# Second layer's gated convolution: the difference and the gate product move from GpSimd to VectorE, the first tap from VectorE to ScalarE, and two tiles stand ahead of the softmax

## The chip, the cores and the metric

One core of a Trainium2 chip runs the whole program. The metric is the time of one execution on the device in microseconds (us). Below, PE is TensorE, DVE is VectorE, ACT is ScalarE, POOL is GpSimd and SP is SyncE; all numbers are float32.

## What is computed

Two layers, one after the other, work on 4 x 512 tokens of width 128. The change lies in the second layer's mixer, which works on 256 hidden channels:

```python
    u = jnp.einsum('bld,hd->blh', x, W_x) + b_x
    g = jax.nn.sigmoid(jnp.einsum('bld,hd->blh', x, W_g) + b_g)
    h = conv(u, conv_w) + conv_b            # per channel, 3 taps along the tokens
    u = u * g + h * (1.0 - g)
    dt = softplus(einsum('bld,hd->blh', x, W_dt) + b_dt).mean(axis=(0, 1)); dt = clip(dt, 0.001, 2.0)
    A = -softplus(A_raw)
    A_d = exp(A * dt[:, None]); B_d = (A_d - 1.0) / (A + 1e-06) * B_ssm
    # state = A_d * state + B_d * u_t ; y_t = sum(state * C_ssm)
    y = scan(u); return layernorm(x + y @ W_out.T + b_out)
```

Beside the mixer, the second layer has a mixture of 8 experts (softmax gate, best two of eight), and the result is the sum of both and of the input.

## The kernel before

The second layer is one block of the program (`layer1`), in which each engine has its own list of instructions written out by hand; counters (semaphores) hold an engine until another has come far enough. Nothing is reordered: what stands first on an engine runs first.

The tokens are worked on in `NU` = 8 tiles, n = 0 to 7: batch row n // 2 (512 tokens, along the free dimension) and half n % 2 of the 256 channels (on 128 partitions). For one tile:

- PE makes u, the gate and dt products (`u_product`, `gate_product`, `dt_product`).
- ACT copies u from PSUM into `ub` with its bias (`u_tile`, L1564), makes the gate by a sigmoid (L1589), and for dt an absolute value and a relu (L1599, L1602; a softplus in two parts).
- DVE makes the convolution in `cv`, one instruction for each tap (`conv`: L1716, L1718, L1721), and, later in its list, the sum `uT = cv + df` (`blend`, L1728).
- POOL stands between the two: `df = ub - cv` (L1867) and `df = df * gate` (L1870).

`ub`, `cv` and `df` have two places each, used in turn. The profile shows them all as "region", since they are parts of one tensor.

Around the tiles, DVE's list holds the gates of the experts (`gates`: softmax, best two; L1672 to L1691), four copies (`gate_rows`, L1696) and products with the gates of the experts (`apply_gate`, L1701). The order before is: conv(0), conv(1), gates, blend(0), then for n = 2 to 7 conv(n) and blend(n - 1) with the smaller pieces between, and blend(7) last. Then come two transposes of all of `uT` (L1755), and a chain of short instructions that makes dt (L1758 to L1765) and `lna` (L1766), the logarithm of the state's decay. It needs the end of the softplus from ACT (`ln_done`, raised at L1618). For `lna` the rest waits: on ACT, exponentials (L1620, L1622) and then the activations of the next experts (`hidden`, L1557), on PE the products of these experts (`up`, L1396, `picks`, `down`), and after them the matrices of the scan (L1631 to L1646).

POOL's list in this block is: clear `gt` (L1858), add a bias to `xt` (L1861), the eight pairs L1867 and L1870, add `out_b` to `xn1` (L1871), clear region2 once `ln_done` is 2 (L1873), and at the very end parts of the last sums.

Of the kernel before, what the change touches and what calls it, by code (L numbers as in the profile page):

```python
# [11 lines left out]
ACT = mybir.ActivationFunctionType  # L12
ALU = mybir.AluOpType
# [3 lines left out]
B, L, D = 4, 512, 128  # L17
# [80 lines left out]
def build(nc, a, const, out):  # L98
    ctx = ExitStack()
    with ctx, nc.allow_non_contiguous_dma(reason="bias columns and token regrouping"):  # L100
# [39 lines left out]
        with ExitStack() as until_layer1:  # L140
# [1144 lines left out]
def layer1(nc, a, out, g):  # L1285
# [13 lines left out]
    a_raw, b_ssm, c_ssm, cw, cb = m1.a_raw, m1.b_ssm, m1.c_ssm, m1.cw, m1.cb  # L1299
    NBC = B * NCH  # L1300
    NU = 2 * B
    with ExitStack() as c:
        uT = sb("uT", [P, 2, TOK], c=c)
# [5 lines left out]
        gate = region1[:, :].rearrange("p (n l) -> p n l", n=NU)  # L1309
# [9 lines left out]
        ub = region3[:, 0:W].rearrange("p (n l) -> p n l", n=2)  # L1319
        cv, df = (region3[:, W + 2 * L * i:W + 2 * L * (i + 1)].rearrange("p (n l) -> p n l", n=2) for i in range(2))  # L1320
# [23 lines left out]
        S = lambda *names: tuple(sem(n, c) for n in names)  # L1344
# [1 line left out]
            "gate_mm", "mx_done", "ex_done", "gates_done", "gt_mm", "gT_done", "moe_order")  # L1346
        up_mm, pick_mm, he_done, gated, down_mm, y_done = S("e_up", "e_pick", "he_done", "gated", "e_down", "y_done")
        w_mm, w_done, pads, u_mm, g_mm, dt_mm = S("mix_tr", "mix_cp", "pads", "u_mm", "g_mm", "dt_mm")
        u_done, gate_done, conv_done, diff_done, blend_in, uT_done = S(
            "u_done", "gate_done", "conv_done", "diff_done", "blend_in", "uT_done")  # L1350
        abs_done, relu_done, exp_done, ln_done = S("abs_done", "relu_done", "exp_done", "ln_done")

        a_stage, lna_done, t1_done, kex_stage = S("a_stage", "lna_done", "t1_done", "kex_stage")
# [11 lines left out]
        row = lambda b: slice(b * L, (b + 1) * L)  # L1365
# [19 lines left out]
        with nc.Block() as block:  # L1385
# [165 lines left out]
            def _(act):  # L1551
# [7 lines left out]
                def u_tile(n):  # L1559
                    act.wait_ge(u_mm, n + 1)  # L1560
                    if n >= 2:
                        act.wait_ge(conv_done, 3 * (n - 1))
                        act.wait_ge(diff_done, n - 1)
                    nc.scalar.activation(ub[:, n % 2, 1:L + 1], bank[n % 2][:, :], ACT.Identity, bias=m1.bx[:, n % 2:n % 2 + 1]).then_inc(u_done, 1)  # L1564

                def tap_blocks(q):

                    nc.scalar.activation(wtap[quad(q), :, quad(q)], x2[quad(q), :, :].rearrange("p c j -> p j c"),  # L1568
                                         ACT.Copy).then_inc(taps, 1)
# [26 lines left out]
                for n in range(NU):  # L1596
                    b, k = divmod(n, 2)
# [66 lines left out]
            def _(dve):  # L1664
# [29 lines left out]
                def gate_rows(k):  # L1694
                    dve.wait_ge(gt_mm, k + 1)
                    nc.vector.tensor_copy(gT[:, k * 512:(k + 1) * 512], bank[6 + k % 2][:, :]).then_inc(gT_done, 1)  # L1696

                def apply_gate(n):
                    dve.wait_ge(he_done, n + 1)
                    dve.wait_ge(pick_mm, n + 1)  # L1700
                    nc.vector.tensor_tensor(he[:, n % 8, :], he[:, n % 8, :], pick_bank(n // 4, n % 4)[:, :], ALU.mult).then_inc(gated, 1)  # L1701
# [6 lines left out]

                def conv(n):

                    b, k = divmod(n, 2)
                    p = n % 2
                    dve.wait_ge(u_done, n + 1)
                    if n >= 2:
                        dve.wait_ge(uT_done, n - 1)
                    nc.vector.tensor_scalar(cv[:, p, :], ub[:, p, 0:L], cw[:, k, 0:1], cb[:, k:k + 1], ALU.mult, ALU.add).then_inc(conv_done, 1)  # L1716
                    dve.wait_ge(conv_done, 3 * n + 1)
                    nc.vector.scalar_tensor_tensor(out=cv[:, p, :], in0=ub[:, p, 1:L + 1], scalar=cw[:, k, 1:2], in1=cv[:, p, :],  # L1718
                                                   op0=ALU.mult, op1=ALU.add).then_inc(conv_done, 1)
                    dve.wait_ge(conv_done, 3 * n + 2)  # L1720
                    nc.vector.scalar_tensor_tensor(out=cv[:, p, :], in0=ub[:, p, 2:L + 2], scalar=cw[:, k, 2:3], in1=cv[:, p, :],  # L1721
                                                   op0=ALU.mult, op1=ALU.add).then_inc(conv_done, 1)

                def blend(n):

                    b, k = divmod(n, 2)
                    dve.wait_ge(blend_in, n + 1)
                    nc.vector.tensor_tensor(uT[:, k, row(b)], cv[:, n % 2, :], df[:, n % 2, :], ALU.add).then_inc(uT_done, 1)  # L1728


                sc = Chain(dve, v_order)
# [4 lines left out]
                nc.vector.tensor_tensor(asp[:], asp[:], a_raw[:], ALU.max).then_inc(a_stage, 1)  # L1736
                w(nc.vector.tensor_scalar(bsp[:], a_raw[:], 0.0, None, ALU.max))
                conv(0)
                conv(1)
                gates()  # L1740
                blend(0)
                for n in range(2, NU):
                    conv(n)
                    blend(n - 1)
                    if n in (2, 3):
                        gate_rows(2 * n - 4)
                        gate_rows(2 * n - 3)
                    if n >= 6:
                        apply_gate(2 * n - 12)
                        apply_gate(2 * n - 11)  # L1750
                blend(NU - 1)
                dve.wait_ge(uT_done, NU)
                for i in range(2):
                    half_n = slice(i * NBC // 2, (i + 1) * NBC // 2)
# [55 lines left out]
                for m in range(8):  # L1810
# [3 lines left out]
                    n = 512 - (m == 7)  # L1814
# [41 lines left out]
            @block.gpsimd  # L1856
            def _(pool):
                nc.gpsimd.memset(gt, 0.0).then_inc(pool_stage, 1)  # L1858
                pool.wait_ge(m1.w_in, 16 * m1.loads)

                nc.gpsimd.tensor_tensor(xt[:], xt[:], m1.lnb[:, None, :].broadcast_to([P, NT, D]), ALU.add).then_inc(pool_stage, 1)  # L1861
                for n in range(NU):
                    p = n % 2
                    pool.wait_ge(conv_done, 3 * n + 3)
                    if n >= 2:
                        pool.wait_ge(uT_done, n - 1)
                    nc.gpsimd.tensor_tensor(df[:, p, :], ub[:, p, 1:L + 1], cv[:, p, :], ALU.subtract).then_inc(diff_done, 1)  # L1867
                    pool.wait_ge(diff_done, n + 1)
                    pool.wait_ge(gate_done, n + 1)
                    nc.gpsimd.tensor_tensor(df[:, p, :], df[:, p, :], gate[:, n, :], ALU.mult).then_inc(blend_in, 1)  # L1870
                nc.gpsimd.tensor_tensor(xn1[:], xn1[:], m1.out_b[:, None, :].broadcast_to([P, NT, D]), ALU.add).then_inc(pool_stage, 1)  # L1871
                pool.wait_ge(ln_done, 2)
                nc.gpsimd.memset(region2[:], 0.0).then_inc(pool_stage, 1)  # L1873
                for m in range(2):
                    scale_add(nc, pool, m)
# [35 lines left out]
```

## Time and profile before

| | |
|---|---|
| median of 3 runs | 486.31 us (486.05 to 487.7) |
| the profiled execution's own time | 487.49 us |
| its span, from first to last instruction | 485.7 us, so 1.79 us lie around it |
| second layer's block | about 332 us to 485.7 us of the span |
| busy in the span: PE, DVE, ACT, POOL | 390.9, 307.6, 291.9, 196.3 us |
| mean granted clock of PE | 0.911 of full speed |

The profile lists for every instruction when it ran, how long, and what its engine had waited for. A duration includes time in which an instruction had begun and could not proceed. Two instructions on one engine overlap by some 0.1 us when the second does not need the first's result, so the distance between two starts is often a little less than the duration.

### The profile page before, as it was taken

The page shows a single profiled execution, that of the slowest core. Times are in us where ns is not written, and L with a number is a line of the kernel's source. Part 1 is how long each engine was busy: PE and PEld are TensorE (multiplying, and loading weights), DVE is VectorE, ACT ScalarE, POOL GpSimd, SP SyncE. Part 2 cuts the span into 40 slices and gives each one's busy share as a digit, 9 for nine tenths or more (in the row PEclk, how much of TensorE's full clock was granted, in tenths as well). Part 3 has the DMA queues.
Part 4 walks back from the last instruction along what each step waited for, and adds up shares of the span by engine and source line. Part 5 has one row for each costly group of instructions (what it writes and reads, how often), then busy time and mean ns, then how long its engine had stood idle before and what let it go on. Part 6 is the DMA issues. An engine that isn't in the chain of part 4 may idle for free. (4 is left out here: it accounts for less than half of the span.)

```text
span 485.7 us, 10292 instructions
## 1 busy us (share of the span) xinstructions
PE 390.9 (80%) x3168; PEld 266.0 (55%) x3168; DVE 307.6 (63%) x1066; ACT 291.9 (60%) x707; POOL 196.3 (40%) x279
## 2 busy tenths in 40 slices
PE   0799999986999999999970999973898456785990
PEld 0443444335777777777750577762543142665890
DVE  4664726333777777777761357777489896365096
ACT  1266858583666677666651446663578925696634
POOL 1001736403588888888863600005415760000003
PEclk9999999998899999999995579995899876997996
DMA  8120223243122222222123510000000001000003
GB/s 232 22 49 28 67 68 98 69 120 119 42 57 62 65 60 64 65 65 65 49 84 90 118 21 1 2 0 1 0 1 1 1 0 23 1 1 1 0 1 86
DMA packets 35355, 23.06 MB, mean 47 GB/s; under 512 B 10478, under 2 KB 35068, under 8 KB 35324
## 3 DMA queue, kind: packets, MB, share of 16 engines
q1 hardware_dynamic: 34908, 22.55, 17.3%
q8 instruction: 15, 0.25, 0.2%
q10 hardware_dynamic: 416, 0.13, 0.1%
q14 instruction: 16, 0.13, 0.1%
HBM read 13.20 MB, written 9.47 MB: 47 GB/s over the span
## 5 line engine op out<-in xcount | busy, mean ns | idle before, releaser
L449 PE MATMUL bank<-w,hT 128*128 128x385 f32 x128 | 45.6, 496 | 0.6 <-ACT stage L577 0.6
L906 ACT ACTIVATE win<-bank 128x384 f32<-128x384 f32 (+1 forms) x124 | 43.1, 399 | 0.0
L835 PE MATMUL bank<-win,wst 128*32 128x128 f32 x1024 | 42.7, 282 | 0.0
L449 PEld LDWEIGHTS bank<-w,hT 128*128 128x128 f32 x128 | 23.2, 189 | 25.0 <-issue 12.7
L1167 ACT ACTIVATE std_<-mv_,cst 128x2 f32<-128x2 f32 (+1 forms) x46 | 13.5, 296 | 37.2 <-DVE mv_ L1147 20.3
L1380 POOL TENSOR_TENSOR win<-win,lng 128x512 f32<-128x512 f32 x2 | 2.5, 1265 | 77.1 <-ACT win L1661 77.1
L835 PEld LDWEIGHTS bank<-win,wst 128*32 128x32 f32 x1024 | 25.3, 110 | 8.0 <-issue 0.6
L1396 PE MATMUL bank<-xn1T,w1e 128*128 128x512 f32 x32 | 17.7, 676 | 12.4 <-ACT he L1557 12.1
L973 POOL TENSOR_SCALAR xh<-raw,bmv,brs 128x128 f32<-128x128 f32 x32 | 25.4, 793 | 3.0 <-DVE brs L1025 2.9
L830 PE MATMUL bank<-win,cst 128*128 128x128 f32 x128 | 25.6, 283 | 0.7 <-DVE grad L1072 0.7
L966 POOL TENSOR_TENSOR xkm<-win,wst 128x256 f32<-128x256 f32 x32 | 19.6, 613 | 15.0 <-PE bank L852 12.7
L911 ACT ACTIVATE zstd<-zmv,cst 128x1 f32<-128x1 f32 x32 | 9.4, 294 | 26.5 <-DVE zmv L1049 26.5
L1858 POOL MEMSET region<- 128x2048 f32 x1 | 1.8, 1806 | 58.2 <-POOLq L1110 58.2
L576 ACT ACTIVATE stage<-bank 128x384 f32<-128x384 f32 x32 | 15.5, 485 | 11.7 <-PE bank L449 11.2
L852 PE MATMUL bank<-grad,xkm 32*128 32x128 f32 x496 | 22.5, 296 | 0.0
L958 POOL TENSOR_TENSOR gd<-wst,win 128x128 f32<-128x128 f32 x32 | 13.8, 432 | 21.4 <-POOLq L295 21.4
L1867 POOL TENSOR_TENSOR region<-region 128x512 f32<-128x512 f32 x8 | 11.9, 1492 | 25.4 <-DVE region L1721 25.4
L1217 PE MATMUL bank<-region,tT 128*128 128x256 f32 x64 | 21.9, 472 | 0.0
L422 DVE TENSOR_TENSOR move<-tw,coup 128x512 f32<-128x512 f32 x8 | 8.7, 1090 | 20.2 <-ACT coup L609 20.2
L1203 PE MATMUL bank<-cst,yn 128*128 128x128 f32 x32 | 8.0, 340 | 16.2 <-ACT yn L1184 14.2
L830 PEld LDWEIGHTS bank<-win,cst 128*128 128x128 f32 x128 | 20.1, 198 | 1.0 <-DVE grad L1072 0.9
L852 PEld LDWEIGHTS bank<-grad,xkm 32*128 32x128 f32 x496 | 16.6, 185 | 3.7
(300 smaller groups left out, 1193.6 us busy)
## 6 DMA issues: line engine op xcount, KB each, us to landing
rows_scratch<-stage SPq DMA_DIRECT2D x32, 192.5 KB
win<-rows_scratch SPq DMA_DIRECT2D x32, 192.5 KB, 2.4
attn_scratch<-ob SPq DMA_DIRECT2D x32, 64.0 KB, 1.6
att<-attn_scratch SPq DMA_DIRECT2D x32, 64.0 KB
xt<-in_L_attn_x SPq DMA_DIRECT2D x4, 256.0 KB, 5.9
out<-win SPq DMA_DIRECT2D x4, 256.0 KB, 2.4
cst<-in_constants SPq DMA_DIRECT2D x1, 535.5 KB, 4.3
w<-in_L_attn_wk SPq DMA_DIRECT2D x2, 128.0 KB, 4.9
```

What stands on the lines that cost most here:

```text
L449: mm = nc.tensor.matmul(rows_bank(i, h)[:, 0:RC], hT[:, k, i * P:(i + 1) * P], w4[:, k, h, :], start=(k == 0), stop=(k == 1))
L576: act.activation(stage[:, i % 2, h, 0:3 * F], src[:, 0:3 * F], ACT.Copy).then_inc(stage_done[h], 1)
L830: nc.tensor.matmul(dst[:, 0:F], con("ident"), w_sb[:, state, 2, :], start=True, stop=False, skip_group_check=True)
L835: mm = nc.tensor.matmul(dst[32 * b:32 * b + 32, 0:F], v[:, at:at + 2 * K], w_sb[:, state, first_slot(b) + h, :], start=False, stop=(h == 1 ...
L852: mm = nc.tensor.matmul(bank[b][:, h * F:(h + 1) * F], xkm[own, p % 2, h, :], grad[own, p % 2, :], start=False, stop=False, skip_group_che ...
L906: nc.scalar.activation(w_sb[:, state, at:at + n, :], bank[b][:, 0:n * F].rearrange("f (h g) -> f h g", h=n), ACT.Copy).then_inc(w_done, 1)
L958: nc.gpsimd.tensor_tensor(gd[:], grf[:], rows[:, p, F:2 * F], ALU.mult).then_inc(gd_done, 1)
L966: nc.gpsimd.tensor_tensor(xkm[:, p % 2, :, :], rows[:, p, 0:F][:, None, :].broadcast_to([P, H, F]), headt[:, :, None].broadcast_to([P, H, ...
L973: nc.gpsimd.tensor_scalar(xh[:], raw[:, p % 2, :], bmv[:, 0:1], brs[:, 0:1], ALU.subtract, ALU.mult).then_inc(xg_done, 1)
L1167: nc.scalar.activation(std[:, p, ks], mv[:, p, ks, 1], ACT.Sqrt, bias=con("eps5")).then_inc(std_done, 1)
L1217: ins = nc.tensor.matmul(dst, tT[:, 1 - p, 0, k * P:(k + 1) * P], wo[:, k, :], start=False, stop=(k == 1))
L1396: nc.tensor.matmul(bank[4 + n % 2][:, :], m1.w1[:, q, :], xn1T[:, tok], start=True, stop=True).then_inc(up_mm, 1)
```

## The change

The first tap is now an activation on ACT, right behind the copy of u, in `u_tile`. DVE makes taps two and three, and then, in the new `blend`, the difference, the product with the gate and the sum, all for the same tile. POOL does nothing for the tiles. Tiles 0 and 1 are finished ahead of `gates`. The counters are renumbered for this.

```diff
@@ ScalarE, u_tile(n)
                     if n >= 2:
-                        act.wait_ge(conv_done, 3 * (n - 1))
-                        act.wait_ge(diff_done, n - 1)
+                        act.wait_ge(conv_done, 2 * (n - 1))
+                        act.wait_ge(diff_done, 2 * n - 3)
                     nc.scalar.activation(ub[:, n % 2, 1:L + 1], bank[n % 2][:, :], ACT.Identity, bias=m1.bx[:, n % 2:n % 2 + 1]).then_inc(u_done, 1)
+                    act.wait_ge(u_done, n + 1)
+                    if n >= 2:
+                        act.wait_ge(uT_done, n - 1)
+                    nc.scalar.activation(cv[:, n % 2, :], ub[:, n % 2, 0:L], ACT.Identity, bias=cb[:, n % 2:n % 2 + 1],
+                                         scale=cw[:, n % 2, 0:1]).then_inc(tap_done, 1)
@@ VectorE, conv(n): the first tap goes, the other two stay
-                    dve.wait_ge(u_done, n + 1)
-                    if n >= 2:
-                        dve.wait_ge(uT_done, n - 1)
-                    nc.vector.tensor_scalar(cv[:, p, :], ub[:, p, 0:L], cw[:, k, 0:1], cb[:, k:k + 1], ALU.mult, ALU.add).then_inc(conv_done, 1)
+                    dve.wait_ge(tap_done, n + 1)
...
@@ VectorE, blend(n)
-                    dve.wait_ge(blend_in, n + 1)
-                    nc.vector.tensor_tensor(uT[:, k, row(b)], cv[:, n % 2, :], df[:, n % 2, :], ALU.add).then_inc(uT_done, 1)
+                    dve.wait_ge(conv_done, 2 * n + 2)
+                    nc.vector.tensor_tensor(df[:, p, :], ub[:, p, 1:L + 1], cv[:, p, :], ALU.subtract).then_inc(diff_done, 1)
+                    dve.wait_ge(diff_done, 2 * n + 1)
+                    dve.wait_ge(gate_done, n + 1)
+                    nc.vector.tensor_tensor(df[:, p, :], df[:, p, :], gate[:, n, :], ALU.mult).then_inc(diff_done, 1)
+                    dve.wait_ge(diff_done, 2 * n + 2)
+                    nc.vector.tensor_tensor(uT[:, k, row(b)], cv[:, p, :], df[:, p, :], ALU.add).then_inc(uT_done, 1)
@@ VectorE, the order
                 conv(0)
+                blend(0)
                 conv(1)
+                blend(1)
                 gates()
-                blend(0)
                 for n in range(2, NU):
                     conv(n)
-                    blend(n - 1)
+                    blend(n)
...
-                blend(NU - 1)
@@ GpSimd
-                for n in range(NU):
-                    p = n % 2
-                    pool.wait_ge(conv_done, 3 * n + 3)
-                    if n >= 2:
-                        pool.wait_ge(uT_done, n - 1)
-                    nc.gpsimd.tensor_tensor(df[:, p, :], ub[:, p, 1:L + 1], cv[:, p, :], ALU.subtract).then_inc(diff_done, 1)
-                    pool.wait_ge(diff_done, n + 1)
-                    pool.wait_ge(gate_done, n + 1)
-                    nc.gpsimd.tensor_tensor(df[:, p, :], df[:, p, :], gate[:, n, :], ALU.mult).then_inc(blend_in, 1)
```

The lists of the engines show it as follows (the changed kernel has its own line numbers). First GpSimd's list, before, with the last of the eight pairs (the other seven stand ahead of it, and the clearing L1858 and the addition L1861 ahead of them):

```order
L1867 TENSOR_TENSOR region<-region 128x512 [waits uT_done,conv_done]
L1870 TENSOR_TENSOR region<-region 128x512 [waits gate_done,diff_done]
L1871 TENSOR_TENSOR xn<-xn,out_b 128x2048
L1873 MEMSET region 128x4096 [waits ln_done]
L1380 TENSOR_TENSOR win<-win,lng 128x512 [waits zn_done]
```

And GpSimd's list in the changed kernel, from the block's first clearing on:

```order
L1864 MEMSET region 128x2048
L1867 TENSOR_TENSOR xt<-xt,lnb 128x2048 [waits l1_weights]
L1868 TENSOR_TENSOR xn<-xn,out_b 128x2048
L1870 MEMSET region 128x4096 [waits ln_done]
L1380 TENSOR_TENSOR win<-win,lng 128x512 [waits zn_done]
```

The addition of `out_b` has moved up to right behind the addition to `xt`, with no wait between them, and the clearing of region2 now waits for `ln_done` alone.

Next ScalarE's list from tile 6's copy of u to the first exponential of the softplus, before:

```order
L1564 ACTIVATE region<-bank,bx 128x512 [waits diff_done,conv_done,u_mm]
L1557 ACT_TABLE_LOAD
L1557 ACTIVATE he<-bank,b1e 128x512 [waits e_up] x2
L1564 ACTIVATE region<-bank,bx 128x512 [waits diff_done,conv_done,u_mm]
L1557 ACTIVATE he<-bank,b1e 128x512 [waits e_up] x2
L1613 ACT_TABLE_LOAD
L1613 ACTIVATE region<-region 128x4096 [waits abs_done]
```

And the same place in the changed kernel:

```order
L1564 ACTIVATE region<-bank,bx 128x512 [waits diff_done,conv_done,u_mm]
L1568 ACTIVATE region<-region,cb,cw 128x512 [waits uT_done,u_done]
L1557 ACT_TABLE_LOAD
L1557 ACTIVATE he<-bank,b1e 128x512 [waits e_up] x2
L1564 ACTIVATE region<-bank,bx 128x512 [waits diff_done,conv_done,u_mm]
L1568 ACTIVATE region<-region,cb,cw 128x512 [waits uT_done,u_done]
L1557 ACTIVATE he<-bank,b1e 128x512 [waits e_up] x2
L1618 ACT_TABLE_LOAD
L1618 ACTIVATE region<-region 128x4096 [waits abs_done]
```

Each copy of u is followed by a tap (L1568), with no table load between; everything behind, the softplus included, stands one instruction further back per tile.

Last VectorE's list at the end of the tiles, from conv(7) to the sum in which `ln_done` is waited for, before:

```order
L1716 TENSOR_SCALAR region<-region,cw,cb 128x512 [waits uT_done,u_done]
L1718 SCALAR_TENSOR_TENSOR region<-region,cw 128x512 [waits conv_done]
L1721 SCALAR_TENSOR_TENSOR region<-region,cw 128x512 [waits conv_done]
L1728 TENSOR_TENSOR uT<-region 128x512 [waits blend_in]
L1701 TENSOR_TENSOR he<-he,bank 128x512 [waits e_pick,he_done] x2
L1728 TENSOR_TENSOR uT<-region 128x512 [waits blend_in]
L1755 STREAM_TRANSPOSE region<-uT 128x64x32 [waits uT_done]
L1755 STREAM_TRANSPOSE region<-uT 128x64x32
L1758 TENSOR_REDUCE dt<-dtr 128x2
L1761 TENSOR_TENSOR asp<-bsp,asp 128x32 [waits a_stage,ln_done,ssm_v]
```

And the same place in the changed kernel:

```order
L1718 SCALAR_TENSOR_TENSOR region<-region,cw 128x512 [waits tap_done]
L1721 SCALAR_TENSOR_TENSOR region<-region,cw 128x512 [waits conv_done]
L1729 TENSOR_TENSOR region<-region 128x512 [waits conv_done]
L1732 TENSOR_TENSOR region<-region 128x512 [waits gate_done,diff_done]
L1734 TENSOR_TENSOR uT<-region 128x512 [waits diff_done]
L1706 TENSOR_TENSOR he<-he,bank 128x512 [waits e_pick,he_done] x2
L1761 STREAM_TRANSPOSE region<-uT 128x64x32 [waits uT_done]
L1761 STREAM_TRANSPOSE region<-uT 128x64x32
L1764 TENSOR_REDUCE dt<-dtr 128x2
L1767 TENSOR_TENSOR asp<-bsp,asp 128x32 [waits a_stage,ln_done,ssm_v]
L1768 TENSOR_TENSOR dt<-dt,dtl 128x2
L1769 TENSOR_SCALAR asp<-asp 128x32 [waits ssm_v]
```

A tile is now five instructions of which each needs the one before it, and the last sum no longer stands alone ahead of the transposes.

## Rows read from the trace of the kernel before

**Rows 1.** Chain of work that ended last: start us, us, what.

```profile
388.18 5.02 DVE uT L1728
...
405.06 5.68 PE bank L1396 x8
```

**Rows 2.** Timeline of GpSimd in the second layer: start us, us, instruction.

```profile
332.75 1.81 POOL L1858 MEMSET region<- 128x2048 f32 x1 [58.18 <-POOLq L1110]
334.52 4.49 POOL L1861 TENSOR_TENSOR xt<-xt,lnb 128x2048 f32<-128x2048 f32 x1
...
373.59 1.33 POOL L1870 TENSOR_TENSOR region<-region 128x512 f32<-128x512 f32 x1
...
388.12 4.52 POOL L1871 TENSOR_TENSOR xn<-xn,out_b 128x2048 f32<-128x2048 f32 x1
392.58 3.50 POOL L1873 MEMSET region<- 128x4096 f32 x1
```

**Rows 3.** Timeline of VectorE, 333 to 402 us.

```profile
333.86 0.72 DVE L1735 TENSOR_SCALAR asp<-a_raw 128x32 f32<-128x32 f32 x1
334.62 4.43 DVE L1736 TENSOR_TENSOR asp<-asp,a_raw 128x32 f32<-128x32 f32 x1
...
344.01 0.75 DVE L1718 SCALAR_TENSOR_TENSOR region<-region,cw 128x512 f32<-128x512 f32 x1
344.80 0.75 DVE L1721 SCALAR_TENSOR_TENSOR region<-region,cw 128x512 f32<-128x512 f32 x1
...
352.52 0.29 DVE L1672 TENSOR_REDUCE mx<-bank 128x16 f32<-128x128 f32 x1 [3.17 <-PE bank L1483]
...
359.39 0.69 DVE L1728 TENSOR_TENSOR uT<-region 128x512 f32<-128x512 f32 x1
...
366.95 0.68 DVE L1728 TENSOR_TENSOR uT<-region 128x512 f32<-128x512 f32 x1
367.55 1.28 DVE L1696 COPY ffnT<-bank 128x512 f32<-128x512 f32 x2
...
373.83 1.64 DVE L1718 SCALAR_TENSOR_TENSOR region<-region,cw 128x512 f32<-128x512 f32 x1
...
400.27 0.14 DVE L1758 TENSOR_REDUCE dt<-dtr 128x2 f32<-128x8 f32 x1
...
400.77 0.18 DVE L1763 TENSOR_SCALAR asp<-asp 128x32 f32<-128x32 f32 x1
...
401.26 0.19 DVE L1766 TENSOR_TENSOR lna<-asp,dt 128x32 f32<-128x32 f32 x1
```

**Rows 4.** Waits of the second layer: who waited for whom, total us, times, longest.

```profile
ACT t L1620 <- DVE lna L1766: 10.2, 1, 10.2
...
ACT region L1564 <- POOL region L1867: 2.4, 2, 1.4
```

**Rows 5.** Timeline of ScalarE: first layer (53 to 56 us), then the second.

```profile
53.87 0.69 ACT L603 ACTIVATE tanh<-bank,half_b 128x512 f32<-128x512 f32 x1
54.59 0.81 ACT L609 ACTIVATE coup<-tanh,alpha,beta 128x512 f32<-128x512 f32 x1
55.31 0.47 ACT L576 ACTIVATE stage<-bank 128x384 f32<-128x384 f32 x1
...
369.05 0.69 ACT L1564 ACTIVATE region<-bank,bx 128x512 f32<-128x512 f32 x1
369.62 0.69 ACT L1599 ACTIVATE region<-bank,bd 128x512 f32<-128x512 f32 x1
...
389.83 0.19 ACT L1618 ACTIVATION_READ_ACCUMULATOR region<-region 128x1 f32 x1
...
430.58 1.98 ACT L1568 ACTIVATE region<-region 32x1024 f32<-32x1024 f32 x1
```

**Rows 6.** Windows: length, busy us of PE, PEld, DVE, ACT, POOL (instructions), granted PE clock, DMA.

```profile
396.00:399.00 3.00, 0.00 (x0) 0.00 (x0) 3.00 (x2) 0.00 (x0) 0.09 (x1) 0.97 0.00 0
...
405.00:409.00 4.00, 3.94 (x5) 1.80 (x6) 3.77 (x10) 1.39 (x4) 0.00 (x0) 0.50 0.13 45
```

More of the change, by code:

```diff
@@ L1348, in layer1 @@
         w_mm, w_done, pads, u_mm, g_mm, dt_mm = S("mix_tr", "mix_cp", "pads", "u_mm", "g_mm", "dt_mm")
-        u_done, gate_done, conv_done, diff_done, blend_in, uT_done = S(
-            "u_done", "gate_done", "conv_done", "diff_done", "blend_in", "uT_done")
+        u_done, gate_done, conv_done, diff_done, tap_done, uT_done = S(
+            "u_done", "gate_done", "conv_done", "diff_done", "tap_done", "uT_done")
         abs_done, relu_done, exp_done, ln_done = S("abs_done", "relu_done", "exp_done", "ln_done")
@@ L1709, in conv @@
                 def conv(n):
-                    b, k = divmod(n, 2)
-                    p = n % 2
-                    dve.wait_ge(u_done, n + 1)
-                    if n >= 2:
-                        dve.wait_ge(uT_done, n - 1)
-                    nc.vector.tensor_scalar(cv[:, p, :], ub[:, p, 0:L], cw[:, k, 0:1], cb[:, k:k + 1], ALU.mult, ALU.add).then_inc(conv_done, 1)
-                    dve.wait_ge(conv_done, 3 * n + 1)
+                    k, p = n % 2, n % 2
+                    dve.wait_ge(tap_done, n + 1)
                     nc.vector.scalar_tensor_tensor(out=cv[:, p, :], in0=ub[:, p, 1:L + 1], scalar=cw[:, k, 1:2], in1=cv[:, p, :],
                                                    op0=ALU.mult, op1=ALU.add).then_inc(conv_done, 1)
-                    dve.wait_ge(conv_done, 3 * n + 2)
+                    dve.wait_ge(conv_done, 2 * n + 1)
                     nc.vector.scalar_tensor_tensor(out=cv[:, p, :], in0=ub[:, p, 2:L + 2], scalar=cw[:, k, 2:3], in1=cv[:, p, :],
@@ L1726, in blend @@
                     b, k = divmod(n, 2)
-                    dve.wait_ge(blend_in, n + 1)
-                    nc.vector.tensor_tensor(uT[:, k, row(b)], cv[:, n % 2, :], df[:, n % 2, :], ALU.add).then_inc(uT_done, 1)
+                    p = n % 2
+                    dve.wait_ge(conv_done, 2 * n + 2)
[5 more added lines that the diff above has]
+                    nc.vector.tensor_tensor(uT[:, k, row(b)], cv[:, p, :], df[:, p, :], ALU.add).then_inc(uT_done, 1)
                 sc = Chain(dve, v_order)
@@ L1861, in _ @@
                 nc.gpsimd.tensor_tensor(xt[:], xt[:], m1.lnb[:, None, :].broadcast_to([P, NT, D]), ALU.add).then_inc(pool_stage, 1)
-                for n in range(NU):
-                    p = n % 2
-                    pool.wait_ge(conv_done, 3 * n + 3)
-                    if n >= 2:
-                        pool.wait_ge(uT_done, n - 1)
-                    nc.gpsimd.tensor_tensor(df[:, p, :], ub[:, p, 1:L + 1], cv[:, p, :], ALU.subtract).then_inc(diff_done, 1)
-                    pool.wait_ge(diff_done, n + 1)
-                    pool.wait_ge(gate_done, n + 1)
-                    nc.gpsimd.tensor_tensor(df[:, p, :], df[:, p, :], gate[:, n, :], ALU.mult).then_inc(blend_in, 1)
                 nc.gpsimd.tensor_tensor(xn1[:], xn1[:], m1.out_b[:, None, :].broadcast_to([P, NT, D]), ALU.add).then_inc(pool_stage, 1)
```

## The prediction

> **What bounds the kernel now.** I read the chain of work that ended last first. Through the tiles it is GpSimd's two instructions of each tile and the DVE work between them; then one DVE sum, 0.68 us long elsewhere [rows 3], stands for 5.02 us [rows 1]. The timeline of GpSimd says why: the addition of out_b began at 388.12 and ran 4.52 us [rows 2], just ahead of that sum at 388.18. The same shows in the small: a tap that takes 0.75 us alone took 1.64 us from 373.83, while GpSimd's product ran from 373.59 for 1.33 us [rows 2, 3]. So DVE instructions that read two tensors stand still while a GpSimd tensor_tensor runs. The table of waits says what hangs on the tiles: ACT had been idle for 10.2 us when lna came [rows 4], written from 401.26 [rows 3]. From there the chain goes to PE at 405.06 [rows 1] and on, through PE, ACT and DVE in turn, to the end, each step released by the one before. Lna's time is thus the time of all that follows, and I ask when lna is written in the changed kernel.
>
> **The change, on DVE.** A tile is five dependent instructions. Tap to its dependent is 344.80 - 344.01 = 0.79 us; a tensor_tensor to its dependent is 0.68 + 0.04 (the gap between these taps) = 0.72; to an independent one 367.55 - 366.95 = 0.60 [rows 3]. So tap, tap, difference, product, sum: 0.79 + 0.79 + 0.72 + 0.72 + 0.60 = 3.62 us, now that no GpSimd work lies beside it. The softmax starts at 352.52, after 3.17 us of waiting for PE's router products [rows 3], which in PE's order follow sigmoids of ACT, and a tap now stands ahead of these: +0.83 us (next paragraph), 353.35. Tiles 0 and 1 lie ahead of it: from about 344.1 (where tap two of tile 0 stood, 344.01 [rows 3], and it waits for ACT's tap) two tiles, 7.24 us, and some 1.3 us of waiting for the first sigmoid, to 352.7. That wait of DVE is what hides them, with 0.6 us to spare; beyond that each us is added in full. Conv(2) thus starts where blend(0) stood, 359.39 [rows 3], plus 0.83 = 360.22. Then six tiles, 21.72 us, and eight small instructions (four copies, four products) of 0.60, 4.80 us: the transposes start at 386.74. From the blend's end to the reduction was 400.27 - (388.18 + 5.02) = 7.07 us [rows 1, 3], so the reduction is at 393.8 instead of 400.27: **6.5 us earlier**.
>
> **The change, on ACT.** The tap has a near twin in the first layer, an activation with scale and bias columns from SBUF, 128x512: 0.81 us, 0.72 after the instruction whose result it needs, and 0.72 ahead of the next [rows 5]. A copy of u alone holds the queue for 369.62 - 369.05 = 0.57 [rows 5]; with its tap 1.44, so +0.87 a tile, or +0.83 where a table load, which does not overlap, follows (1.53 for 0.70). Along ACT's list to the softplus: tap 1 +0.83 and tap 2 +0.83, ahead of the sigmoids; tap 3 hidden in a wait for PE's dt product; tap 4 +0.87; tap 5 +0.75 (0.12 in another wait for PE); taps 6 and 7 +0.83 and +0.86; tap 0 hidden in a wait for PE. That is 4.97. Against it, ACT's two waits for GpSimd go, 2.4 us [rows 4] and twice the 0.12 us of overlap that they broke. So the last accumulator read of the softplus, 389.83 + 0.19 [rows 5], moves to about 390.0 + 2.3 = 392.3 us. That is still ahead of DVE's 393.8, and no tap holds DVE up (tap 6 is the nearest, done at 376.9 for a tile that starts at 377.1).
>
> **The change, on GpSimd.** The addition of out_b moves to about 339.0, behind that to xt [rows 2], and beside it DVE has only one short instruction, not needed until the first tile at 344. The clearing of region2 used to run from 392.58 for 3.50 us [rows 2], beside transposes. Now it starts with ln_done, at 392.4, and ends at 395.9, so it lies on the chain that makes dt and lna. Does a clearing hold DVE up? One row bears on it: the 128x32 tensor_scalar at 333.86 took 0.72 us, and 0.18 elsewhere [rows 3], and it ended (334.58) just as GpSimd's clearing ended (332.75 + 1.81 = 334.56) [rows 2]. I take that: the tensor_scalar L1763, ready 0.50 us after the reduction, at 394.3, stands until about 395.75, a new wait of **1.45 us**. Lna follows 0.49 later, at 396.25, instead of 401.26.
>
> The Trainium skill's page SBUF — State Buffer, section "Who interferes with whom", says that VectorE and GpSimd share a pair of ports under an exclusive lock. A tensor_scalar in a two-port mode meets any GpSimd instruction there, and one with two SBUF inputs only those that read SBUF. By that rule the clearing blocks L1763 but not L1761 and L1762 ahead of it, and lna comes at 396.25; the short tensor_scalar at 333.86 agrees, and nothing here shows the second half. The page ScalarE: Activation LUTs, section "Rules for kernel authors", budgets some 0.3 us and 0.83 ns an element for an activation, an estimate of 0.72 us for a tap; the rows say 0.81, and with 0.72 the sum would be some 0.6 us lower.
>
> **The sum.** -6.5 on DVE, +1.45 behind the clearing: -5.0 us. After lna nothing changes but, it may be, PE's clock. Before, PE had nothing to do after 396, its clock was at 0.97 of 2.4 GHz up to 399, and from 405 to 409 it worked 3.94 us at 1.2 GHz [rows 6]. It now restarts at about 400. I take it to be at 1.2 GHz then too, and nothing gained; at the full clock those 3.94 us would be half as long, -2.0 us at most. The profiled execution would go from 487.49 to 482.5; it stood 1.2 us above the median, and from the median of 486.31 I come to **481.3 us**.
>
> Bounds of the unknown prices. The clearing: 0 (it ran beside transposes with no loss) to 1.45. The tap: 0.69, as the copy of u, to 0.81; below, ln_done comes some 0.8 us earlier, and so the end of the clearing (-0.8). Tiles 0 and 1 ahead of the softmax: 0 to +1. A tap on ACT at 1.98, the longest such row [rows 5], is a rival below. With PE's clock these give 479.3 to 482.5.
>
> **Rivals.**
> 1. *The clearing does not block.* For it: transposes ran beside it. Against it: the tensor_scalar at 333.86. Then DVE decides, -6.5: 479.8 us. Chance 0.12.
> 2. *The early addition starves asp.* DVE's L1736 stood 4.43 us behind the addition to xt [rows 3], and ACT's list begins with its result. If GpSimd's next addition, now right behind, is served first, L1736 waits a further 4.5 us and all of the layer moves: 481.3 + 4.5 = 485.8 us. Against it: the tensor_scalar at 333.86 got in between GpSimd's clearing and the addition behind it. Chance 0.06.
> 3. *ACT becomes the bound: slower.* If a tap cost 1.98 us, as the strided copy at 430.58 [rows 5], 1.17 more each, the six or seven taps that count would put ln_done, and the clearing behind it, 7 to 8 us later: 489 us. It decides from a tap of about 1.6 us on. The twin at 0.81 speaks against it. Chance 0.02.
> 4. *The gain does not carry.* Something behind lna (the round trip of lna through DRAM, a product) was due then anyway: 486.3 us. Against it: ACT's idle 10.2 us ahead of lna, and a chain in which each step starts as the last ends. Chance 0.05.
>
> **How the numbers follow.** Forecast 0.75, rivals 0.12, 0.06, 0.02, 0.05. A difference of 0.3%, 1.46 us, is about what this measurement tells from none. Faster: forecast and rival 1, 0.87. Within: rivals 2 and 4, 0.11. Slower: rival 3, 0.02. The range holds the bounds and rival 1 and, above, 1 us more for tiles 0 and 1 or losses that no row shows: 479.3 to 483.5.
>
> **What would show it.** On DVE, eight tiles of 3.6 us with no tap above 0.8, the transposes at about 386.7, and the tensor_scalar behind them at 1.5 us, ending with the clearing. On ACT, taps of 0.81 us, no wait for GpSimd or VectorE in the tiles, the last accumulator read at 392.3, and the wait for lna about 2.5 us instead of 10.2. On GpSimd, the addition of out_b at 339. Wrong would be: asp written at 343.5 (rival 2); a softmax that starts later than 353.4 (tiles 0 and 1 not covered); a clearing that ends with no DVE instruction behind it (rival 1); or an lna at 396 with a span that is not 5 us shorter (rival 4).

## The result, and the profile after the change

Five runs each (the kernel before has two more than above, and the same median): 482.47 us (481.17 to 483.01) against 486.31 us before (486.05 to 487.7), a ratio of 0.991 with a 95% interval of 0.9889 to 0.9931. The change makes the kernel 3.8 us faster; the forecast was 481.3 us, with a range of 479.3 to 483.5. The profiled execution took 482.47 us too.

The top of the page after the change:

```profile
span 480.7 us, 10286 instructions
...
PE 390.9 (81%) x3168; PEld 265.9 (55%) x3168; DVE 308.6 (64%) x1074; ACT 298.3 (62%) x715; POOL 173.1 (36%) x263
```

GpSimd has 23 us less to do and ACT 6 us more. The chain of work that ended last, from the softplus on (start us, us, what), answers to [rows 1]:

```profile
387.43 3.80 ACT region L1623 x4
...
391.26 1.66 DVE region L1761
...
393.27 1.55 DVE asp L1769
...
395.08 0.20 DVE lna L1772
...
398.14 0.70 ACT he L1557
...
398.88 6.46 PE bank L1396 x8
```

The sum that stood 5.02 us behind GpSimd is gone from it. A clearing's wait (L1769, 1.55 us) is in it now, and the next products of experts on PE, behind lna, take 6.46 us (x8: four products, each with two records). The timeline of GpSimd, as [rows 2]:

```profile
333.28 4.49 POOL L1867 TENSOR_TENSOR xt<-xt,lnb 128x2048 f32<-128x2048 f32 x1
337.73 4.51 POOL L1868 TENSOR_TENSOR xn<-xn,out_b 128x2048 f32<-128x2048 f32 x1
391.27 3.51 POOL L1870 MEMSET region<- 128x4096 f32 x1 [49.03 <-ACT region L1623]
```

And that of VectorE, as [rows 3]: behind the early addition, at the softmax, in a tile, and at the end of the tiles:

```profile
333.38 4.44 DVE L1742 TENSOR_TENSOR asp<-asp,a_raw 128x32 f32<-128x32 f32 x1
337.74 4.53 DVE L1743 TENSOR_SCALAR bsp<-a_raw 128x32 f32<-128x32 f32 x1
...
352.13 0.29 DVE L1677 TENSOR_REDUCE mx<-bank 128x16 f32<-128x128 f32 x1 [0.39 <-PE bank L1483]
...
368.65 0.74 DVE L1718 SCALAR_TENSOR_TENSOR region<-region,cw 128x512 f32<-128x512 f32 x1
369.43 0.75 DVE L1721 SCALAR_TENSOR_TENSOR region<-region,cw 128x512 f32<-128x512 f32 x1
370.22 0.69 DVE L1729 TENSOR_TENSOR region<-region 128x512 f32<-128x512 f32 x1
370.94 0.69 DVE L1732 TENSOR_TENSOR region<-region 128x512 f32<-128x512 f32 x1
371.67 0.69 DVE L1734 TENSOR_TENSOR uT<-region 128x512 f32<-128x512 f32 x1
372.28 0.74 DVE L1718 SCALAR_TENSOR_TENSOR region<-region,cw 128x512 f32<-128x512 f32 x1
...
385.55 7.37 DVE L1761 STREAM_TRANSPOSE region<-uT 128x2048 f32<-128x2048 f32 x2
392.77 0.15 DVE L1764 TENSOR_REDUCE dt<-dtr 128x2 f32<-128x8 f32 x1
392.98 0.19 DVE L1767 TENSOR_TENSOR asp<-bsp,asp 128x32 f32<-128x32 f32 x1
393.09 0.15 DVE L1768 TENSOR_TENSOR dt<-dt,dtl 128x2 f32<-128x2 f32 x1
393.27 1.55 DVE L1769 TENSOR_SCALAR asp<-asp 128x32 f32<-128x32 f32 x1
...
395.08 0.19 DVE L1772 TENSOR_TENSOR lna<-asp,dt 128x32 f32<-128x32 f32 x1
```

A tile takes 372.28 - 368.65 = 3.63 us. L1769 is held until the clearing ends (391.27 + 3.51 = 394.78), while the two-input L1767 and L1768 just ahead of it ran through it unhindered. ScalarE, as [rows 5], and its wait for lna, as [rows 4] (who waited for whom: total us, times, longest):

```profile
370.36 0.69 ACT L1564 ACTIVATE region<-bank,bx 128x512 f32<-128x512 f32 x1
371.08 0.81 ACT L1568 ACTIVATE region<-region,cb,cw 128x512 f32<-128x512 f32 x1
371.80 0.67 ACT L1604 ACTIVATE region<-bank,bd 128x512 f32<-128x512 f32 x1
...
391.03 0.18 ACT L1623 ACTIVATION_READ_ACCUMULATOR region<-region 128x1 f32 x1
```

```profile
ACT t L1625 <- DVE lna L1772: 2.8, 1, 2.8
```

Windows behind lna (columns as in [rows 6]):

```profile
396.00:399.00 3.00, 0.12 (x1) 0.12 (x1) 0.69 (x4) 2.77 (x4) 0.00 (x0) 0.77 0.25 38
399.00:405.00 6.00, 6.00 (x8) 2.30 (x8) 5.21 (x13) 2.37 (x4) 0.00 (x0) 0.54 0.12 27
405.00:409.00 4.00, 4.00 (x32) 2.97 (x32) 0.69 (x1) 0.78 (x2) 0.00 (x0) 1.00 0.00 0
```

And the stretch in which PE's clock fell, ahead of these products:

```profile
397.00:398.00 1.00, 0.00 (x0) 0.00 (x0) 0.00 (x0) 1.00 (x1) 0.00 (x0) 0.82 0.09 33
398.00:399.00 1.00, 0.12 (x1) 0.12 (x1) 0.09 (x1) 0.99 (x3) 0.00 (x0) 0.50 0.49 66
```

The clock is down when PE's work behind lna begins at 398.88, and back within 404 to 405. That is some 5.6 us of work at 1.2 GHz; before it was four [rows 6].

**Where the time went.** The first layer is unchanged, yet its length differs between executions: the second layer's first instruction on VectorE (a memset) stands at 333.03 us before and 331.80 after, and at 330.4 to 333.2 in the profiles below. I therefore count from it. *Lna*: 401.26 - 333.03 = 68.23 us into the layer before, 395.08 - 331.80 = 63.28 after, **-4.95 us**. *Behind lna*, to the end of the span: 485.7 - 401.26 = 84.44 before, 480.7 - 395.08 = 85.62 after, **+1.18 us**. Together -3.77 us, and the medians differ by 3.84. That they agree so well is in part luck: a second measurement of both kernels ("changed, again" below) gave 482.19 against 487.25 us, 5.06 us less, while its profile has lna and the rest where the first had them. The medians alone put the gain between some 3 and 6 us; its terms are read from the profiles.

### The profile page after: what moved, and what is told of

The parts are those of the page before. It is cut to its first block and busy times, and to the rows that moved or that the text cites. A ratio compares the mean times of both kernels' runs of the same rounds, so it can differ in the third digit from the quotient of the medians.

```text
span 480.7 us, 10286 instructions
## 1 busy us (share of the span) xinstructions
PE 390.9 (81%) x3168; PEld 265.9 (55%) x3168; DVE 308.6 (64%) x1074; ACT 298.3 (62%) x715; POOL 173.1 (36%) x263
## 5 line engine op out<-in xcount | busy, mean ns | idle before, releaser
L966 POOL TENSOR_TENSOR xkm<-win,wst 128x256 f32<-128x256 f32 x32 | 19.6, 612 | 14.5 <-PE bank L852 12.4
L1870 POOL MEMSET region<- 128x4096 f32 x1 | 3.5, 3512 | 49.0 <-ACT region L1623 49.0
```

The source lines that it names most:

```text
L966: nc.gpsimd.tensor_tensor(xkm[:, p % 2, :, :], rows[:, p, 0:F][:, None, :].broadcast_to([P, H, F]), headt[:, :, None].broadcast_to([P, H, ...
```

## The experiments

In this table, "lna" is lna's start in us into the second layer, "behind" is from it to the span's end, "1.2 GHz" is PE's busy time behind lna at the lower clock (summed over windows of half a us, from busy time and granted clock; rough). "Lna" and "behind" come from one profile of each kernel. Each ratio is against the kernel before in the same set of runs.

| kernel | median us | ratio (95%) | lna | behind | 1.2 GHz |
|---|---|---|---|---|---|
| before | 486.31 | | 68.23 | 84.44 | 7.0 |
| changed | 482.47 | 0.991 (0.9889 to 0.9931) | 63.28 | 85.62 | 9.3 |
| changed, again | 482.19 | 0.9902 (0.987 to 0.9934) | 63.29 | 85.48 | 9.2 |
| e1: early addition alone | 481.08 | 0.9878 (0.9861 to 0.9896) | 63.73 | 84.45 | 7.1 |
| e2: clearing behind lna | 480.69 | 0.9866 (0.9849 to 0.9884) | 61.88 | 85.75 | 12.2 |
| e3: first tap on VectorE | 482.48 | 0.9915 (0.9891 to 0.9939) | 64.36 | 84.18 | 6.5 |
| e4: blends behind the softmax | 493.35 | 1.0115 (1.0097 to 1.0133) | 73.66 | 85.38 | 8.8 |
| e5: PE kept busy in one wait | 481.69 | 0.9903 (0.9866 to 0.994) | 63.09 | 84.86 | 7.6 |
| e6: late addition | 485.08 | 0.9958 (0.9932 to 0.9984) | 65.03 | 85.61 | 12.4 |
| e7: e1, a transpose behind lna | 480.08 | 0.9865 (0.9823 to 0.9907) | 60.64 | 86.9 | 13.2 |
| e8: changed, PE kept busy | 480.44 | 0.9868 (0.9835 to 0.99) | 63.10 | 83.01 | 0 |
| e9: e7, PE kept busy | 477.01 | 0.9788 (0.9757 to 0.9818) | 60.81 | 82.99 | 1.4 |
| e10: before, PE kept busy | 484.22 | 0.9932 (0.9906 to 0.9957) | 68.22 | 82.99 | 0 |
| e11b: both transposes behind lna | 476.6 | 0.9782 (0.9758 to 0.9807) | 57.62 | 84.34 | 4.2 |

My theory: lna's time sets the end, and it was late because of the addition; the rest of the change gives little more, since the clearing takes a part back. The rivals: the relief of GpSimd in the tiles, or the tap on ScalarE, is what gains. A second question came with the result: is the 1.18 us behind lna PE's clock?

### The addition of out_b alone (e1)

The kernel before, with GpSimd's addition moved ahead of its eight pairs:

```diff
                 nc.gpsimd.tensor_tensor(xt[:], xt[:], ...)
+                nc.gpsimd.tensor_tensor(xn1[:], xn1[:], m1.out_b...)
                 for n in range(NU):
...
-                nc.gpsimd.tensor_tensor(xn1[:], xn1[:], m1.out_b...)
```

> The kernel before, with one line moved: GpSimd adds out_b to xn1 ahead of the eight tiles instead of behind them; all else is as before. My theory (lna sets what follows, and the last sum of the tiles stood behind that addition): the sum needs 0.7 us instead of 5.0, the reduction starts about 4.3 us earlier in the second layer, the clearing now ends before it, lna is 4.3 us earlier, so about 482.0 us against 486.3; 1 us more or less with the time that PE spends at the lower clock after lna. Rival (the gain of the change comes from the 26 us of tiles in which GpSimd held up VectorE): little of it is here, 485 to 486 us.

Measured 481.08 us and lna at 63.73. One moved line brings lna forward by 4.5 us, and its median is no worse than that of the whole change. The clearing now runs under the transposes and ends 2.5 us before they do, so no instruction of the dt chain is held. In its timeline of VectorE:

```profile
386.40 7.30 DVE L1755 STREAM_TRANSPOSE region<-uT 128x2048 f32<-128x2048 f32 x2
393.55 0.15 DVE L1758 TENSOR_REDUCE dt<-dtr 128x2 f32<-128x8 f32 x1
...
394.06 0.18 DVE L1763 TENSOR_SCALAR asp<-asp 128x32 f32<-128x32 f32 x1
```

### The addition late again, in the changed kernel (e6)

```diff
+                pool.wait_ge(uT_done, 7)
                 nc.gpsimd.tensor_tensor(xn1[:], xn1[:], m1.out_b...)
```

> The changed kernel, but GpSimd's addition of out_b waits until tile 6 is blended, so it lies beside tile 7 as in the kernel before. Theory (such an addition stops every VectorE instruction that reads two tensors): the first tap of tile 7 on VectorE, due at 380.7, stands until the addition ends at about 384.1, so the transposes start 3.3 us later; the clearing is then over before the reduction and blocks nothing, which gives 1.4 us back: 2.0 us more than the changed kernel. Rival (the early place is worth nothing by itself): no difference.

It does what it did before the change, now to a tap. GpSimd, then VectorE:

```profile
378.37 4.52 POOL L1869 TENSOR_TENSOR xn<-xn,out_b 128x2048 f32<-128x2048 f32 x1 [41.73 <-DVE uT L1734]
```

```profile
379.40 4.04 DVE L1718 SCALAR_TENSOR_TENSOR region<-region,cw 128x512 f32<-128x512 f32 x1
```

A tap of 0.74 us stands 4.04. The transposes start 3.1 us later than in the changed kernel, lna comes 1.75 later (63.28 to 65.03; 2.0 were expected), since the clearing is then over before the tensor_scalar. The median is 2.9 us worse than the changed kernel's in the same set of runs (482.19 to 485.08). So the addition's place counts in both kernels. But it is not all of the gain: with the addition late, the rest of the change still has lna 3.2 us earlier than the kernel before (68.23 to 65.03). Only on top of an early addition does it give little (63.73 to 63.28).

### The clearing behind lna (e2)

```diff
-                pool.wait_ge(ln_done, 2)
+                pool.wait_ge(lna_done, 1)
                 nc.gpsimd.memset(region2[:], 0.0)
```

> The changed kernel, but GpSimd's clearing of region2 waits for lna instead of for the softplus. Theory (the clearing holds up VectorE's tensor_scalar ahead of lna): this tensor_scalar falls from 1.55 to 0.18 us, lna comes 1.4 us earlier, and the clearing now stands against instructions that have time, so 481.1 us where the changed kernel has 482.5. Rival (something else ended that wait, or the clearing now blocks the chain behind lna as long): 482.5 us or more.

VectorE, then GpSimd:

```profile
393.26 0.18 DVE L1769 TENSOR_SCALAR asp<-asp 128x32 f32<-128x32 f32 x1
...
393.75 0.19 DVE L1772 TENSOR_TENSOR lna<-asp,dt 128x32 f32<-128x32 f32 x1
...
394.75 2.80 DVE L1778 TENSOR_SCALAR asp<-asp 128x32 f32<-128x32 f32 x1
```

```profile
394.00 3.51 POOL L1870 MEMSET region<- 128x4096 f32 x1 [51.70 <-DVE lna L1772]
```

L1769 takes 0.18 us instead of 1.55 and lna comes 1.40 us earlier. The median of 480.69 (481.1 were expected) is 1.5 to 1.8 us below the two medians of the changed kernel; its interval lies clear of the first one's and overlaps with the second one's. The wait moved to the next tensor_scalar, 2.80 us, which is not due. Thus the new wait's price was 1.4 us, and the clearing blocks. The Trainium skill, page SBUF — State Buffer, section "Who interferes with whom", has both halves of this: a tensor_scalar in a two-port mode meets any GpSimd instruction, one with two SBUF inputs only those that read SBUF, and a clearing reads nothing. The changed kernel's trace agrees with the second half too: there L1767 and L1768 took 0.19 and 0.15 us in the clearing's midst.

### The first tap back on VectorE (e3)

```diff
@@ ScalarE, u_tile(n)
-                    nc.scalar.activation(cv[...], ub[...], ACT.Identity, bias=cb..., scale=cw...).then_inc(tap_done, 1)
@@ VectorE, conv(n)
+                    nc.vector.tensor_scalar(cv[...], ub[...], cw..., cb..., ALU.mult, ALU.add).then_inc(tap_done, 1)
```

> The changed kernel with the first tap back on VectorE; the difference and the product stay there, so a tile is six instructions on VectorE. Theory: a tile costs 4.20 instead of 3.62 us, 3.5 us more for the six tiles behind the softmax, which itself starts 0.8 us earlier as ScalarE has no tap ahead of the sigmoids; the softplus ends some 2 us earlier, so the clearing is over before the reduction and blocks nothing, 1.4 us less. Sum +1.3 us on the changed kernel: 483.8. Rival (ScalarE's longer list set the time of the changed kernel, through softplus and clearing): not slower than the changed kernel, 482.5 or less.

Lna is 1.08 us later (64.36), near what was expected, but the median is the same as the changed kernel's, not 1.3 us more, since less is lost behind lna (84.18 instead of 85.62). Without the tap ScalarE's softplus is done 3.1 us earlier and the clearing starts and ends under the transposes. So the tap on ScalarE is worth 64.36 - 61.88 = 2.5 us of lna where the clearing is out of the way, and 1.1 where it is not. And against e1, which has the first tap on VectorE too, the difference and the product on VectorE instead of GpSimd, with tiles 0 and 1 ahead of the softmax, bring lna no gain: 64.36 against 63.73. Both of the rivals fall as the one source of the gain: neither move gives the 4.95 us. As parts they stay, for without the early addition the two moves together are worth 3.2 us (e6).

### Blends of tiles 0 and 1 behind the softmax (e4)

```diff
                 conv(0)
-                blend(0)
                 conv(1)
-                blend(1)
                 gates()
+                blend(0)
+                blend(1)
```

> The changed kernel with the blends of tiles 0 and 1 behind the softmax, as tile 0's stood before. Theory (the order matters more than the placing, since ScalarE's next copy of u waits for the difference of tile 0 and stands ahead of four sigmoids and the whole of the softplus): ScalarE stands still for some 6 us, its whole list and the clearing move by as much, and lna comes about 6 us later: 488 us, slower than the kernel before. Rival (VectorE's own time is what counts, 2.1 us for each of two tiles): 486.7 us at most.

It was 493.35 us, where 488 were expected: the order does matter, and more than I had thought. Its timeline of ScalarE:

```profile
360.53 0.69 ACT L1564 ACTIVATE region<-bank,bx 128x512 f32<-128x512 f32 x1 [6.71 <-DVE region L1729]
361.96 0.81 ACT L1568 ACTIVATE region<-region,cb,cw 128x512 f32<-128x512 f32 x1 [0.74 <-DVE uT L1734]
...
366.94 0.69 ACT L1594 ACTIVATE region<-bank,bg 128x512 f32<-128x512 f32 x1 [1.59 <-PE bank L1455]
368.64 0.69 ACT L1594 ACTIVATE region<-bank,bg 128x512 f32<-128x512 f32 x1 [1.02 <-PE bank L1455]
370.35 0.69 ACT L1564 ACTIVATE region<-bank,bx 128x512 f32<-128x512 f32 x1 [1.02 <-PE bank L1449]
```

Tile 2's copy of u needs the difference of tile 0 (it overwrites `ub`), and stands 6.71 us for it, as the theory had it. Two things I had left out. Its tap waits another 0.74 us for tile 0's sum. And PE, whose products stand behind these sigmoids, had nothing to do for 7.79 us and came back at 1.2 GHz (its granted clock was 0.50 from 364 to 370 us), so that the next sigmoids and the next copy waited for PE. Counted from the layer's start, the tap is 7.4 us later than in the changed kernel, the next copy of u 10.0, and lna 10.4. The two tiles ahead of the softmax fill a wait of VectorE, and they also keep ScalarE and PE running.

### Is the loss behind lna PE's clock? (e5, e8, e10)

Products of which nothing is used (128x512, into a free bank) go into PE's waits. In e5 six of them stand behind `down(0)`, ahead of the products that wait for lna:

```diff
                     down(t - 1)
+                    if t == 1:
+                        for _ in range(6):
+                            nc.tensor.matmul(bank[1][:, :], con("ident"), xn1T[:, 0:512], start=True, stop=True)
```

> The changed kernel, with six products that nothing uses (128x512, into a free bank) on PE behind the first down product, in the 5.8 us in which PE waits for the experts' activation behind lna. Theory (PE worked 5.6 us at 1.2 GHz behind lna in the changed kernel, against 4.0 before, and that gave 0.8 us of the gain back): PE keeps 2.4 GHz through the wait, the expert products take 3.6 instead of 6.5 us, and VectorE's products with the gates set what follows, so the picks start 1.1 us earlier: 1.1 us less than the changed kernel. Rival (the clock there is off the path): no difference.

```profile
397.94 3.89 PE L1396 MATMUL bank<-xn1T,w1e 128*128 128x512 f32 x8 [0.54 <-ACT he L1560]
```

The four products behind lna took 3.89 us instead of 6.46, and the next step on PE (L1407, the picks) began 9.10 us behind lna instead of 10.19, as expected. But PE's clock fell again some 19.5 us behind lna (0.69 in 413 to 414 us, 0.50 in 414 to 416), and the median (481.69, interval 0.9866 to 0.994) can't be told from the changed kernel's: inconclusive by itself. So in e8 the changed kernel has such products in all four long waits behind lna (6, 1, 2 and 5 of them):

> The changed kernel with unused products on PE in four waits behind lna (6 behind the first down product, 1 ahead of the third picks, 2 ahead of the third down product, 5 ahead of the scan's output; each 128x512, 0.86 us at 2.4 GHz), all into banks that are free and each group shorter than its wait. Theory (the time from lna to the end, 85.6 us in the changed kernel against 84.4 before, is longer by PE's time at 1.2 GHz there, 9.3 us of busy time against 7.0): with 0 to 2 us at 1.2 GHz that time falls to 82.5 to 83.5 us and the kernel by 2 to 3 us. Rival (the clock's time is off the path or falls again elsewhere, as when only the first wait was filled): 85 us or more from lna to the end.

and in e10 the kernel before has them too (10, 1, 2 and 5):

> The kernel before, with the same unused products (10, 1, 2 and 5, as its first wait is 9.8 us). lna stays at 68.2 us into the layer. Theory (clock and lna are separate terms): from lna to the end falls from 84.4 to 82.5 to 83.5 us, so 1 to 2 us less than before. Rival (the clock costs only where lna is early): no difference.

Windows of e8:

```profile
396.00:399.00 3.00, 2.49 (x7) 0.94 (x6) 1.07 (x2) 2.40 (x3) 0.00 (x0) 1.00 0.27 55
399.00:405.00 6.00, 5.44 (x23) 2.09 (x22) 4.79 (x13) 2.75 (x4) 0.00 (x0) 1.00 0.09 16
...
438.00:442.00 4.00, 4.00 (x39) 4.00 (x38) 0.00 (x0) 2.15 (x2) 0.00 (x0) 1.00 0.00 0
```

The granted clock stays at 2.4 GHz, and from lna to the end it is 83.01 us in e8 and 82.99 in e10, by one profile each: equal. The 1.18 us between before and changed are gone when the clock is held, so it was the clock that made them. In the second layer the two differ only in lna then, 68.22 - 63.10 = 5.1 us. The medians are a coarser witness. E8's is 1.8 to 2.0 us below the changed kernel's, where the profiles give 2.6. E10's is 2.8 us below that of the kernel before, with an interval of 2.1 to 4.6, and the 1.5 us of the profiles lie outside it; their spans do differ by 2.8 us, but 1.3 of these lie in the unchanged first layer. Whether that is chance was not settled.

### Towards a faster kernel (e7, e9, e11b)

Lna needs neither of the transposes ahead of it. e7 is e1 with the second one later:

```diff
-                for i in range(2): (transpose of half i of uT)
+                turn(0)
                 w(nc.vector.tensor_reduce(dt[:], dtr[:], AX, ALU.add))
...
+                turn(1)
                 add_experts(1)
```

> The kernel before with the early addition (as the first experiment) and, on VectorE, the second transpose moved behind the chain that makes lna, to where VectorE waits for the experts (ahead of the second addition of experts). Theory (lna sets what follows, and it needs no transpose, only the softplus, which ends at 387.5 there): lna comes 3.6 us earlier less 0.5 us for which the clearing holds the tensor_scalar, and the second transpose lies in a wait of 3.9 us: 478.0 us where the first experiment had 481.1. Rival (the products of the experts ahead of lna, which end at 394.2, hold up those behind it, or the transpose holds up what it stands ahead of): 480 us or more.

Lna came 3.1 us earlier than in e1, as expected, but the time is only 1.0 us better, 480.08 where 478.0 were expected and the rival had 480 or more: 2.45 us were lost behind lna. One of the windows of e7 where it went:

```profile
402.00:407.00 5.00, 5.00 (x32) 5.00 (x32) 3.64 (x2) 0.00 (x0) 0.00 (x0) 0.66 0.00 0
```

PE was busy for 13.2 us at 1.2 GHz. To see whether the clock or the moved transpose costs it, e9 adds unused products to e7 (1, 1, 2 and 5):

> The kernel of the experiment with lna between the transposes, with unused products on PE in four waits (1, 1, 2 and 5 of 128x512). There lna came 60.6 us into the layer, but 86.9 us passed from lna to the end, 13.2 us of PE's busy time of it at 1.2 GHz. Theory: from lna to the end falls to 82.5 to 84 us, 3 us less than without the products, 477 us and the fastest of all. Rival (something other than the clock made that time longer, such as the transpose that was moved into it): 86 us or more.

From lna to the end it is 82.99 us again, and the median is 477.01, as expected: the transpose costs nothing that shows where it stands, and the 3.9 us go with the clock. The last kernel, e11b, is e9 without the first unused product, with `turn(0)` behind the dt chain too and the clearing behind the second transpose (v_done 2):

```diff
-                turn(0)
                 w(nc.vector.tensor_reduce(dt[:], dtr[:], AX, ALU.add))
...
                 w(nc.vector.reciprocal(asp[:], asp[:]))
+                turn(0)
...
-                pool.wait_ge(ln_done, 2)
+                pool.wait_ge(v_done, 2)
                 nc.gpsimd.memset(region2[:], 0.0)
```

> The kernel of before with the addition of the output bias ahead of the blends, both transposes of the second half behind the softplus chain, the clearing behind the last tile, and unused products in three of TensorE's waits. First theory (the multiplied numbers' wait sets the end, term by term): the result lna comes at about 58.0 us into the second layer instead of 60.8 in the kernel with only the second transpose moved; the first transpose then delays the picks, so that the stretch from lna to the end grows by about 1 us to 84; in sum 475.3 us, a ratio near 0.976. Rival: the down projection of the first expert (ending 63.5 us into the layer) or the transposes set the picks, and the stretch grows by all that lna gained: 477 us or more.

Its timeline of VectorE:

```profile
387.37 0.19 DVE L1769 TENSOR_TENSOR asp<-bsp,asp 128x32 f32<-128x32 f32 x1 [1.04 <-ACT region L1626]
...
388.16 0.19 DVE L1774 TENSOR_TENSOR lna<-asp,dt 128x32 f32<-128x32 f32 x1
...
389.75 3.74 DVE L1763 STREAM_TRANSPOSE region<-uT 128x2048 f32<-128x2048 f32 x1
```

Lna is set by ScalarE's softplus now, at 57.62 us, and 84.34 us follow: both terms as expected. But the median of 476.6 lies between the theory's 475.3 and the rival's 477: the profiled execution, at 474.33 us, was the fastest of five, and the median can't be told from e9's 477.01 by their intervals. From the layer's start to the end e11b's profile is 1.8 us shorter than e9's (142.0 against 143.8); by the medians it is 0.4 us. Whether it is the faster of the two is not settled. Both beat the kernel before by 2.1 to 2.2% and the changed one by 5 to 6 us.

## Why the prediction was right, and where its sum was off

Step by step, with the times from the layer's first instruction on VectorE (333.03 us before), so that the forecast's times can be compared:

- *Softmax.* Forecast at 353.35 (20.32 us in), measured 20.33, with 0.39 us of wait left of 3.17: tiles 0 and 1 just fit. e4 shows what their place is worth: 10.4 us of lna, far more than VectorE's own queue would tell.
- *Transposes and reduction.* Forecast 53.71 and 60.8 us in, measured 53.75 and 60.97. The tile of 3.62 us held, and so did the reading of the 5.02 us (e1, e6).
- *ScalarE.* Tap 0.81 us. The last accumulator read ends at 59.41 us in, forecast 59.3. Its wait for lna: 2.8 us, forecast about 2.5.
- *The clearing.* Forecast a new wait of 1.45 us; L1769 stood 1.55 - 0.18 = 1.37 longer, and e2 gives 1.40 for it. (The forecast lets the instruction stand until about 395.75 and the clearing end at 395.9; by its own argument both end together. This moves the sum by less than 0.1 us.)
- *Lna.* Forecast -5.0 us, measured -4.95; 5.1 between e10 and e8.
- *Rivals.* 1 falls by the clearing's wait. 2 falls: L1742 took 4.44 us, as before, and the early addition held only L1743 (4.53 us), which nothing needed soon. 3 falls by the tap's 0.81. 4, in full, falls by e8 and e10: behind lna it is the same 83.0 us with the clock held.
- *The step that was off* is "After lna nothing changes but, it may be, PE's clock [...] I take it to be at 1.2 GHz then too, and nothing gained", with -2.0 us as the bound. The clock was indeed at 1.2 GHz, but for longer than before: the term was +1.2 us, outside the bounds I had set at 0 and -2.0. With it the sum is 481.3 + 1.2 = 482.5 us, which is the median. I had looked at whether the clock would be low when PE restarts, and not at how long it stays low.
- *Luck.* The profiled execution was forecast at 482.5 and took 482.47, but in it the second layer began 1.23 us earlier than in the profile before, which no one forecast and which happens to cancel the 1.18 us lost behind lna. Nor are the bounds a full sum of their terms: 481.3 with 1 us for tiles 0 and 1 is 482.3, not 482.5, and a clearing that costs nothing together with a full clock would have been some 477.9, below the range. The measured 482.47 lies just above the named terms, inside the 1 us that was allowed for losses that no row shows.

The gain's sources, as lna's time: 4.5 us for the addition alone (e1), 3.2 for all the rest without it (e6), 4.95 for both. So they don't add up to one split. A part of this is the clearing, which runs under the transposes in e1 and e6 and costs 1.4 us in the changed kernel: with it out of the way both together give 6.35 us (e2). Whoever moves the addition alone has nearly all of what the change gives as it stands.

Left open: why the clock came back after some 4 us of work in one kernel and after 5.6 in the other, and why the intermediate kernels (e2, e6, e7) have 12 to 13 us of work at 1.2 GHz. That they do is read; what decides it was not tried.

## What to carry to other kernels

Before moving work between engines, look for one long GpSimd instruction that holds VectorE up just ahead of the last step (here an addition of 4.5 us): moving that alone may give nearly all that the redistribution gives. When a step comes earlier, ask which instruction it now meets (here a clearing that used to lie under transposes), and count from a result to the end separately from what comes before it. Where PE waits some microseconds on a critical chain, give the clock a term of its own, which can come out as a gain or as a loss; a few unused products in the waits take it out, and here that was worth 1.5 (e10), 2.6 (e8) and 3.9 us (e9) by the profiles.

## What the runs showed of the hardware

- What PE's clock costs after a wait was not one fixed price here. Before, PE had nothing to do for some 10 us, its mean granted clock was 0.68 in 396 to 404 us, and it was back at 2.4 GHz at 409, 4 us after PE's restart. In the changed kernel the wait was 5.67 us, the clock was full up to 397 us, fell within 397 to 398 (0.82), was at 0.50 when PE restarted at 398.88, and then stayed down for some 5.6 us of work. The shorter wait was the dearer one.
- A VectorE instruction held by one GpSimd instruction was not held by the next, though the two stand back to back: L1742, held by the addition to xt, ended at 337.82 us, while the next addition, begun at 337.73, ran on to 342.24. L1743 behind it then stood for 4.53 us.
- A tensor_scalar of 0.18 us stood up to 2.80 us behind a clearing (e2), while two transposes beside a clearing took 7.30 (e1), 7.27 (e3) and 7.37 us (changed), and 7.34 us with no clearing beside them (e2): no sign of a loss for these.
